# Attention scores for the first batch: four units abreast over six PSUM banks, with masks, maxima and side work put in another order

## The chip, the cores and the metric

The kernel runs on one core of a Trainium2 chip. The metric is the device time of one execution in microseconds (us). Three runs of the kernel before gave 480.39, 482.08 and 484.3 us, with a median of 482.08 us.

## The reference, cut to what matters

The program is one transformer block over 4 batches of 512 tokens of width 256: a modulated layer norm, causal attention with 16 heads of width 16, a gated residual, a second modulated layer norm, and a mixture of 8 experts (one per token) with a shared expert beside them. The change touches the attention of the first batch alone, and what is prepared for the second while it runs:

```python
h = _layernorm(x) * (1 + ca) + sa
qkv = jnp.einsum('bsh,oh->bso', h, Wqkv) + bqkv
scores = jnp.einsum('bhqd,bhkd->bhqk', q, k) * scale      # 16 heads, 512 x 512, causal
scores = jnp.where(causal, -jnp.inf, scores)
attn = jax.nn.softmax(scores, axis=-1)                    # needs each row's maximum
out = jnp.einsum('bhqk,bhkd->bhqd', attn, v)
```

The modulation vectors `sa, ca, ga, sb, cb, gb` are rows of `silu(c) @ wmod`.

## The kernel before, in words

**Two passes over the scores.** The kernel first computes the scores with queries on partitions, only to take each row's maximum (DVE, line 1097). The negated maxima are then written into two spare rows of the stacked queries `qs`, so that a second product, with keys on partitions (`scores_t`, line 1573, matmul at 1592), gives scores minus maximum at once, and ACT takes the exponential (line 872). A *unit* is one PSUM bank of first-pass scores: a query tile t of 128 rows (with 128(t+1) keys), a head i of its group, and m heads in one bank. A group of four heads has 11 units, a batch 4 groups, so 44 units. The first pass runs `LAG` = 33 units ahead of the second.

**The order is written out.** Each engine walks the same loop, `for b in range(-1, B)` and in it `n` from 0 to 43. Stage b = -1 is the head: there the first 33 units of batch 0 are computed by `scores_apart` (line 1517) and nothing of the second pass. Beside them each engine does side work at the steps that the table `HEAD` (line 99) gives, in the order of its own loop. `v` is a projection of V, `turn` the transposes of the next batch's normalised rows, `qk` its four projections of Q and K (units 0 to 3, line 1499), `max` the transpose of the maxima (line 1569) and their negation on DVE (line 1101). `SPLITS` (line 91) says at which step ACT and DVE split a piece of the expert weights into a high and a low half.

**Unstacked products.** For batch 0 the stacked operands arrive late, so `scores_apart` multiplies the four 32-row parts of `qk0` by `qz`, the queries masked to even or odd heads. A mask matmul (L1536, 128x128, all 128 rows) opens each tile and three products of 32 rows (L1541) follow; two units are worked alternately, on different 32-row groups of the array. Units rotate over four banks (`s_bank`, line 275); before a bank is used again, PE waits until DVE has taken the maximum of the unit that was in it (`s_mx`, function `before`, line 279). `query_parity` (line 1257) makes `qz` on DVE, eight instructions (L1261).

**What is precomputed, and where.** PE turns the normalised rows (line 1492). ACT writes them with the modulation as a high half and in f32 (`h_parts`, line 838, L847). POOL subtracts for the low half (`h_low`, line 715, L719). PE projects. ACT writes high half and f32 (`qk_parts`, line 850, L861), and POOL again subtracts (`qk_low`, line 721, L726). `project_qk` waits for both halves of h. PE takes bank M1 for side work in order, each job waiting for the release of the last (`take_bank`, line 1486). POOL works strictly in order too. At steps 30 and 36 of the head it makes the gate rows out of the modulation (`modulation_rows`, line 695, called at line 773), ahead of the side jobs of the same step:

```python
if b < 0 and n in (30, 36):
    modulation_rows(n == 36)
for job, c, k in side_jobs(b, n):      # "turn" -> h_low, "qk" -> qk_low
```

**The SP queue** issues its DMAs in one order, each waiting in front of all behind it. For this stretch the order is:

```python
qk_out(1, 0)          # waits for the high, then the low halves of qk(1,0) and qk(1,1): 6 DMAs
maxima_out(0, 0); maxima(0, 0)
stacks(1, 0)          # waits for qk_out(1, 0) to land: 4 DMAs
qk_out(1, 1); stacks(1, 1)
for k in range(2): halves_out(k); stage_load(k + 3)
```

The first three `stage_load` come ahead of it, and the first of them waits for `s_mp`, since the expert weights overwrite the modulation weights. On ACT, `split_high(2)` (line 911) stands at step 4 of stage b = 0; it waits for the landing of `halves_out(0)` (line 542), which frees its buffer.

Of the kernel before, what the change touches and what calls it, by code (L numbers as in the profile page):

```python
# [20 lines left out]
P = 128  # L21
# [44 lines left out]

def key_units():

    return [(0, i, 1) for i in range(4)] + [(1, i, 1) for i in range(4)] + [(2, 0, 2), (2, 2, 2), (3, 0, 4)]
# [21 lines left out]
SPLITS = {-1: {24: 0, 36: 1},  # L91
# [22 lines left out]
def build(nc, x, wqkvT, bqkv, bqkc, woutT, bout, rwT, gup, down, sgw, suw, sdw, cT, wmod, out):  # L114
    ctx = ExitStack()
    with ctx:
# [158 lines left out]
        def s_bank(N):  # L275

            return [S0, S1, T2, OTb][N % 4] if N < LAG else [T2, S0, S1][N % 3]

        def before(N):

            return max((n + 1 for n in range(max(N - 4, 0), N) if s_bank(n) is s_bank(N)), default=0)
# [40 lines left out]
        s_qz = sem("s_qz")  # L322
        s_tile = sem("s_tile")
# [82 lines left out]
        QU, KU = query_units(), key_units()  # L406
# [57 lines left out]
        def _(sp):  # L464
# [173 lines left out]
        def _(po):  # L638
# [127 lines left out]
            h_low(0, 1)  # L766
            for u in range(4):
# [58 lines left out]
        def _(ac):  # L826
# [118 lines left out]
            def modulation_rows():  # L945
                ac.wait_ge(s_mp, 1)
                ac.wait_ge(s_wl, 1)
                for c, bk in enumerate((T0, T1)):
                    a.activation(mraw[:, 512 * c:512 * (c + 1)], bk[0:B, :], ACT.Copy).then_inc(s_mr, 1)

            for b in range(-1, B):
                for n in range(BU):
# [3 lines left out]
                    if b < 0 and n == 15:  # L956
                        modulation_rows()
# [68 lines left out]
        def _(ve):  # L1026
# [61 lines left out]
            def maxima(N):  # L1088

                b, gr = N // BU, N % BU // UNITS  # L1090
                t, i, m = QU[N % UNITS]
# [165 lines left out]
            def query_parity(f, c):  # L1257

                ve.wait_ge(*((s_ql, 2 * f + 1) if c else (s_qh, 2 * f + 1)))
                for par in range(2):  # L1260
                    v.tensor_scalar(qz[:, c, f, par], qk0[:, c, f], pick[:, par:par + 1], None,  # L1261
                                    ALU.mult).then_inc(s_qz, 1)
# [12 lines left out]
            for c in range(2):  # L1275
                query_parity(1, c)
            for b in range(-1, B):
                for n in range(BU):
# [5 lines left out]
                    if b < 0 and n == 14:  # L1284
                        v.memset(ks[1].rearrange("p h n -> p (h n)").bitcast(F32), ONES).then_inc(s_zero, 1)
                    if b < 0 and n == 22:
# [169 lines left out]
        def _(pe):  # L1456
# [18 lines left out]
            def modulation_rows(c):  # L1475
                pe.wait_ge(s_wmr, 16)
                pe.wait_ge(s_q32, 4)
                for k in range(KC):
                    i = t_.matmul([T0, T1][c][0:B, :], cs[:, 1, k], wm[:, k, 512 * (c + 1):512 * (c + 2)],
                                  start=(k == 0), stop=(k == KC - 1))  # L1480
                if c == 1:
                    i.then_inc(s_mp, 1)
# [34 lines left out]
            def scores_apart(pair):  # L1517

                gr = pair[0] // UNITS
                par, f = gr % 2, gr // 2  # L1520
                t, _, m = QU[pair[0] % UNITS]
                w = P * (t + 1)
                if pair[0] == 0:
                    pe.wait_ge(s_const, 2)
                    pe.wait_ge(s_col, 1)
                if pair[0] % (2 * UNITS) == 0:
                    pe.wait_ge(s_qz, 4 * f + 4)
                    pe.wait_ge(s_ql, 2 * f + 2)
                if max(before(N) for N in pair):
                    pe.wait_ge(s_mx, max(before(N) for N in pair))  # L1530
                for i in range(m):
                    c = slice(w * i, w * (i + 1))
                    if i:
                        pe.wait_ge(s_tile, n_tile[0])
                    for N in pair:
                        t_.matmul(s_bank(N)[:, w * (i + 1) - P:w * (i + 1)], identb[:, :], maskb[:, :],  # L1536
                                  start=(i == 0), stop=False, skip_group_check=True)
                    for p, (cq, ck) in enumerate(((0, 0), (0, 1), (1, 0))):
                        for N in pair:
                            j = 32 * (QU[N % UNITS][1] + i)  # L1540
                            q = t_.matmul(s_bank(N)[:, c], qz[j:j + 32, cq, f, par, P * t:w],  # L1541
                                          qk0[j:j + 32, 2 + ck, f, 0:w], start=False,
                                          stop=(p == 2 and i == m - 1), skip_group_check=True)
                            if p == 2 and i == m - 1:
                                q.then_inc(s_s1, 1)
                    if i < m - 1:
# [26 lines left out]
            def scores_t(N):  # L1573
# [7 lines left out]
                if N == 0:  # L1581
                    pe.wait_ge(s_mr, 2)
# [13 lines left out]
            def values(G, j):  # L1596
# [4 lines left out]
                if j == 0:  # L1601
                    pe.wait_ge(*((s_ote, G) if G else (s_mx, LAG)))
# [102 lines left out]
            for b in range(-1, B):  # L1705
                for n in range(BU):
# [189 lines left out]
```

## Time and profile before

| what | value |
|---|---|
| median of three runs | 482.08 us |
| the profiled execution | 481.26 us |
| its span | 479.5 us |
| PE busy | 414.1 us (86%) |
| DVE busy | 317.1 us (66%) |
| ACT busy | 226.7 us (47%) |
| POOL busy | 210.3 us (44%) |

The span runs from the first to the last instruction of the core; the profiled execution took 1.76 us more than it. Busy time is the union of an engine's instructions. The chain that ended last gives 55% of the span to PE, 17% to DVE, 7% to POOL, 6% to ACT, 5% to DMA and 2% to the SP queue.

### The profile page before, as it was taken

Reading aid. Unit: us, or ns where it says so; the run is one execution under the profiler, and the core shown is the slowest. Engines: PE = TensorE matmul, PEld = TensorE weight load, DVE = VectorE, ACT = ScalarE, POOL = GpSimd, SP = SyncE. Lnnn points to the kernel's source line nnn. Section 1 sums busy time; section 2 is a strip of 40 time slices with the busy share of each in tenths; the row PEclk is TensorE's granted clock in tenths of the full one; section 3 lists DMA queues with packets and bytes.
Section 4 is the critical chain, followed back from the end, with each engine's and each line's share of the span. In section 5 each row is a group of like instructions: output and inputs, shape, how many; then the busy total and the mean of one; then the engine's idle time right before and its main releaser. Section 6 shows DMA issues by size and latency. Waiting matters only on the chain.

```text
span 479.5 us, 8593 instructions
## 1 busy us (share of the span) xinstructions
PE 414.1 (86%) x3009; PEld 230.8 (48%) x3009; DVE 317.1 (66%) x639; ACT 226.7 (47%) x403; POOL 210.3 (44%) x251
## 2 busy tenths in 40 slices
PE   4699983989987888997898969999998999999991
PEld 4234332334544344553443426557655666666661
DVE  3796582966797986899986873497954434444441
ACT  2522441687767575665776554526232332323220
POOL 2491670375232782437541582310240464555332
PEclk9988877799999999998999988999999999999997
DMA  7557358755586665855143101598251344434210
GB/s 245 183 144 199 108 119 243 261 187 170 133 259 232 212 187 136 204 173 176 39 139 125 47 0 45 181 387 310 85 179 45 65 72 91 72 80 73 41 21 0
DMA packets 45921, 67.97 MB, mean 142 GB/s; under 512 B 5364, under 2 KB 33652, under 8 KB 45880
## 3 DMA queue, kind: packets, MB, share of 16 engines
q1 hardware_dynamic: 40200, 58.76, 39.7%
q0 software_dynamic: 5152, 8.14, 8.6%
q8 instruction: 26, 0.43, 0.4%
q10 hardware_dynamic: 528, 0.52, 0.3%
q14 instruction: 15, 0.12, 0.1%
HBM read 43.14 MB, written 25.18 MB: 142 GB/s over the span
## 4 chain that ended last, share of the span: by engine, by line
PE 55%; DVE 17%; POOL 7%; issue 6%; ACT 6%; DMA 5%; SPq 2%; ACTq 0%; DVEq 0%; POOLq 0%
PE bank L1463 35%; PE bank L1608 4%; DVE mx L1097 4%; PE bank L1592 3%; PE bank L1829 2%; DVE rowg L1198 2%; PE bank L1563 2%; PE bank L1541 2%; POOL W L745 2%; ACT W L847 2%; DMA w_d<-rowg 2%; DMA mod_d<-h2T 1%; POOL rowg L753 1%; POOL rowg L752 1%; DMA qk_d<-W 1%
## 5 line engine op out<-in xcount | busy, mean ns | idle before, releaser
L872 ACT ACTIVATE W<-bank 128x512 f32<-128x512 f32 (+1 forms) x176 | 94.8, 563 | 64.4 <-PE bank L1592 62.9
L1097 DVE TENSOR_REDUCE mx<-bank 128x1 f32<-128x384 f32 (+3 forms) x176 | 105.7, 633 | 19.1 <-PE bank L1565 11.3
L1463 PE MATMUL bank<-W 128*128 128x256 f16 (+2 forms) x756 | 107.9, 295 | 8.2 <-POOL W L719 3.6
L1463 PEld LDWEIGHTS bank<-W 128*128 128x128 f16 x756 | 73.6, 100 | 43.5 <-issue 15.2
L745 POOL TENSOR_SCALAR_AFFINE_SELECT W<-W 128x512 f32<-128x512 f32 x64 | 46.0, 721 | 82.3 <-ACT W L872 82.2
L1592 PE MATMUL bank<-W 128*128 128x512 f16 (+3 forms) x256 | 65.1, 312 | 11.5 <-ACT W L872 9.8
L1463 PE MATMUL bank<-W,h2T 128*128 x276 | 67.2, 380 | 1.8 <-DVE W L1213 1.0
L815 POOL DMA_INDIRECT out<-h2T,sidx x23 | 36.3, 1578 | 64.0 <-DVE h2T L1433 63.7
L1563 PE MATMUL bank<-W 126*128 126x128 f16 (+3 forms) x208 | 54.7, 314 | 6.5 <-DVE mx L1097 6.5
L1608 PE MATMUL bank<-W 128*32 128x128 f32 (+3 forms) x512 | 49.1, 457 | 9.1 <-POOL W L745 8.9
L1592 PEld LDWEIGHTS bank<-W 128*128 128x128 f16 x256 | 22.1, 100 | 48.2 <-ACT W L872 24.5
L1463 PE MATMUL bank<-h2T,W 128*128 128x512 f16 x192 | 43.1, 379 | 0.6 <-DVE W L1213 0.6
L1426 DVE TENSOR_TENSOR W<-bank,W 128x512 f16<-128x512 f32 x23 | 15.9, 692 | 37.4 <-ACT W L1010 37.4
L1010 ACT ACTIVATE W<-bank 128x512 f16<-128x512 f32 x23 | 13.7, 597 | 55.1 <-PE bank L1829 55.1
L1463 PEld LDWEIGHTS bank<-W,h2T 128*128 128x128 f16 x276 | 26.4, 97 | 27.2 <-issue 6.3
L1198 DVE SCALAR_TENSOR_TENSOR rowg<-stage,rowg 128x1024 f16<-128x1024 f32 x18 | 24.7, 1374 | 20.4 <-ACT rowg L922 20.4
L801 POOL DMA_INDIRECT rowg<-h_d,gidx x23 | 23.6, 1027 | 31.4 <-DVE gidx L1376 24.7
L1565 PE MATMUL bank<-maskb,identb 128*128 128x128 bf16 (+2 forms) x143 | 36.2, 253 | 0.0
L861 ACT ACTIVATE W<-bank,bqk 128x512 f16<-128x512 f32 (+1 forms) x32 | 20.2, 685 | 21.3 <-PE bank L1463 21.2
L1463 PEld LDWEIGHTS bank<-h2T,W 128*128 128x128 f16 x192 | 18.4, 98 | 21.9 <-DVE W L1213 1.0
L1563 PEld LDWEIGHTS bank<-W 126*128 126x128 f16 x208 | 19.5, 100 | 18.3 <-DVE mx L1097 11.7
L726 POOL TENSOR_TENSOR W<-W 128x512 f16<-128x512 f32 x16 | 19.7, 1233 | 16.1 <-ACT W L861 15.9
(171 smaller groups left out, 561.4 us busy)
## 6 DMA issues: line engine op xcount, KB each, us to landing
w_d<-rowg SPq DMA_DIRECT2D x18, 512.0 KB, 3.5
W<-w_d SPq DMA_DIRECT2D x18, 512.0 KB, 7.9
stage<-in_gup SPq DMA_DIRECT2D x16, 512.0 KB
qk_d<-W SPq DMA_DIRECT2D x48, 128.0 KB
W<-qk_d SPq DMA_DIRECT2D x32, 192.0 KB, 4.2
stage<-in_down SPq DMA_DIRECT2D x8, 512.0 KB
x_sb<-in_x SPq DMA_DIRECT2D x4, 512.0 KB, 9.0
h_d<-gbb SPq DMA_DIRECT2D x4, 512.0 KB, 5.0
```

What stands on the lines that cost most here:

```text
L745: g.affine_select(out=d, in_=d, compare_op=ALU.is_ge, fill=0.0, base=0, pattern=[[0, 4], [1, P]], channel_multiplier=-1).then_inc(s_msk, 1)
L801: g.indirect_dma_start(rowg[:, r % RG, :], None, h2_d, bass.IndirectOffsetOnAxis(ap=gidx[:, r:r + 1].bitcast(U32), axis=0)).then_inc(s_gr[ ...
L815: g.indirect_dma_start(out.rearrange("b s n -> (b s) n"), bass.IndirectOffsetOnAxis(ap=sidx[:, r:r + 1].bitcast(U32), axis=0), ry[r % YR], ...
L861: a.activation(dst, side_bank("qk", b, u)[:, :], ACT.Identity, bias=bqk[:, 2 * isk + u // 2:2 * isk + u // 2 + 1], scale=1.0 / WS if isk e ...
L872: a.activation(PT[j][:, i:i + m, :], t_bank(N)[:, 0:m * w].rearrange("p (i n) -> p i n", i=m), ACT.Exp).then_inc(s_exp, 1)
L1097: v.tensor_reduce(mx_v[:, b % 2, hp0 // 4, par, i:i + m, t], s_bank(N)[:, 0:m * w].rearrange("p (i n) -> p i n", i=m), AX.X, ALU.max).then ...
L1198: v.scalar_tensor_tensor(split_part(k, 1), staged(k), WS, split_part(k, 0), ALU.mult, ALU.subtract).then_inc(s_el, 1)
L1463: i = t_.matmul(outp, l, r, start=(n == 0), stop=(n == len(prods) - 1), **kw)
L1563: t_.matmul(bk[:, w * i:w * (i + 1)], qs[r][0:P - 2, hp, par, P * t:w], ks[r][0:P - 2, hp, 0:w], start=(i == 0), stop=False, skip_group_ch ...
L1565: t_.matmul(bk[:, 0:m * w].rearrange("p (i n) -> p i n", i=m)[:, :, w - P:w], identb[:, :], maskb[:, :].unsqueeze(1).to_broadcast([P, m, P ...
L1592: q = t_.matmul(t_bank(N)[:, w * i:w * (i + 1)], ks[r][:, hp, P * j:P * (j + 1)], qs[r][:, hp, par, P * j:S], start=True, stop=True)
L1608: q = t_.matmul(OTb[32 * i:32 * i + 32, P * j:S], v1[b % 2][:, c:c + 32], PT[j][:, i], start=(j == 0), stop=(j == TT - 1), tile_position=( ...
```

## The change

`ROUNDS` lists, for each of three calls per group, which tile of which unit is computed beside which. `first_units` turns the order of the units of the first 33 around. `scores_apart` takes up to four units at once; its banks are six. The four masked queries of the second half go from DVE to ACT. The rows of modulation go into bank M0, in two calls that stand further apart. Normalisation of batch 1 leaves the `HEAD` table and stands ahead of the loop on DVE, with its POOL part ahead of `qk_low`. Three fills on DVE move. Two splits of weights move later. `max` of the first half of batch 0 moves from step 34 to 32 and the projections of batch 1 from steps 26, 28, 31, 33 to 34, 36, 39, 42. SP's order of DMAs and the steps of POOL's `modulation_rows` are not in the diff.

```diff
+def first_units():
+    return [(t, i, 1) for t in (3, 2) for i in range(4)] + [(1, 0, 2), (1, 2, 2), (0, 0, 4)]
+
+ROUNDS = {0: [[(0, 0), (1, 0), (2, 0), (3, 0)]], 4: [[(4, 0), (5, 0), (6, 0), (7, 0)]],
+          8: [[(8, 0), (9, 0), (10, 1)], [(8, 1), (9, 1), (10, 0)], [(10, 2)], [(10, 3)]]}
-SPLITS = {-1: {24: 0, 36: 1},
-          0: {4: 2, 9: 3, 14: 4, 19: 5, 23: 6},
+SPLITS = {-1: {38: 0},
+          0: {1: 1, 4: 2, 9: 3, 14: 4, 19: 5, 23: 6},
-HEAD = [(12, "stats1", 1, 0), (16, "v", 0, 0), (17, "norm1", 1, 0), (18, "v", 0, 1), (20, "turn", 1, 0),
-        (22, "turn", 1, 1), (26, "qk", 1, 0), (28, "qk", 1, 1), (31, "qk", 1, 2), (33, "qk", 1, 3),
-        (34, "max", 0, 0)]
+HEAD = [(19, "v", 0, 0), (25, "v", 0, 1), (28, "turn", 1, 0), (30, "turn", 1, 1), (32, "max", 0, 0),
+        (34, "qk", 1, 0), (36, "qk", 1, 1), (39, "qk", 1, 2), (42, "qk", 1, 3)]
...
-            return [S0, S1, T2, OTb][N % 4] if N < LAG else [T2, S0, S1][N % 3]
+            return [S0, S1, T2, T0, T1, OTb][N % 6] if N < LAG else SB[N % 3]
...
-            head = {"turn": [M1, M0], "qk": [M1, M0, T0, T1]}
+            head = {"turn": [M1, M0], "qk": [M1, M0, T1, OTb]}
...
                 if k == 0:
-                    sp.wait_ge(s_mp, 1)
+                    sp.wait_ge(s_mp, 2)
...
             h_low(0, 0)
             h_low(0, 1)
+            rstd(ve1, mv1, rs1, 1, s_mv, s_rstd)
             for u in range(4):
                 qk_low(0, u)
...
+            query_parity(0)          # on ACT: four activations with a column as scale
+            query_parity(1)
             for b in range(-1, B):
...
-                    if b < 0 and n == 15:
-                        modulation_rows()
+                    if b < 0 and n == 16:
+                        modulation_rows(0)
+                    if b < 0 and n == 22:
+                        modulation_rows(1)
                         other_high()
...
+            v.memset(qs[0].rearrange("p h two n -> p (h two n)").bitcast(F32), 0.0)
             stats1(0)
             parity_columns()
             norm1(0)
+            v.memset(ks[0].rearrange("p h n -> p (h n)").bitcast(F32), ONES).then_inc(s_zero, 1)
             modulation_columns()
             low_qkv()
-
-            v.memset(qs[0].rearrange("p h two n -> p (h two n)").bitcast(F32), 0.0)
+            v.memset(ks[1].rearrange("p h n -> p (h n)").bitcast(F32), ONES).then_inc(s_zero, 1)
+            stats1(1)
+            norm1(1)
             ve.wait_ge(s_pick, 1)
-            query_parity(0, 0)
-            v.memset(ks[0].rearrange("p h n -> p (h n)").bitcast(F32), ONES).then_inc(s_zero, 1)
-            query_parity(0, 1)
-            for c in range(2):
-                query_parity(1, c)
+            query_parity(0)
+            query_parity(1)
...
-                    if b < 0 and n == 22:
+                    if b < 0 and n == 36:
                         low_others()
...
+                rounds = [[(N0 - N0 % UNITS + u, i) for u, i in r] for r in ROUNDS[N0 % UNITS]]
+                units = [N for N, _ in rounds[0]]
...
+                if max(before(N) for N in units):
+                    pe.wait_ge(s_mx, max(before(N) for N in units))
+                left = {N: score_unit(N)[2] for N in units}
+                for k, r in enumerate(rounds):
+                    if k:
                         pe.wait_ge(s_tile, n_tile[0])
+                    for N, i in r:
                         t_.matmul(s_bank(N)[:, w * (i + 1) - P:w * (i + 1)], identb[:, :], maskb[:, :],
...
                     for p, (cq, ck) in enumerate(((0, 0), (0, 1), (1, 0))):
+                        for N, i in r:
...
+                            q = t_.matmul(s_bank(N)[:, w * i:w * (i + 1)], qz[j:j + 32, cq, f, par, P * t:w],
+                                          qk0[j:j + 32, 2 + ck, f, 0:w], start=False, stop=done, skip_group_check=True)
...
                 if N == 0:
-                    pe.wait_ge(s_mr, 2)
+                    pe.wait_ge(s_mx, LAG - 3)
...
                     if 0 <= N < LAG:
-                        if N % UNITS == 0:
-                            scores_apart([N])
-                        elif N % UNITS % 2:
-                            scores_apart([N, N + 1])
+                        if N == 0:
+                            scores_apart(0)
+                        if N % UNITS == 1:
+                            scores_apart(N + 3)
+                        elif N % UNITS == 5:
+                            scores_apart(N + 3)
+                        elif N % UNITS == 9 and N + 2 < LAG:
+                            scores_apart(N + 2)
...
-                    if b < 0 and n in (12, 14):
-                        modulation_rows(n == 14)
+                    if b < 0 and n in (14, 20):
+                        modulation_rows(n == 20)
```

## Rows read from the trace of the kernel before

**Rows 1.** The timeline of PE (start us, us, engine, line, operation), after the head.

```profile
66.50 0.61 PE L1592 MATMUL bank<-W 128*128 128x512 f16 x1
...
83.00 0.50 PE L1592 MATMUL bank<-W 128*128 128x384 f16 x1 [7.62 <-ACT W L872]
```

**Rows 2.** The timeline of ACT, the high half of weight piece 2.

```profile
81.51 1.06 ACT L922 ACTIVATE rowg<-stage 128x1024 f16<-128x1024 f32 x1 [9.72 <-DMA w_d<-rowg]
```

**Rows 3.** The timeline of SP's queue, its DMA issues.

```profile
32.34 3.67 SPq L488 DMA_DIRECT2D qk_d<-W  x6
39.60 1.77 SPq L505 DMA_DIRECT2D W<-qk_d  x4
...
52.66 3.65 SPq L488 DMA_DIRECT2D qk_d<-W  x6
61.12 0.34 SPq L515 DMA_DIRECT2D ng_d<-negm  x1
...
65.08 3.66 SPq L488 DMA_DIRECT2D qk_d<-W  x6
73.71 1.77 SPq L505 DMA_DIRECT2D W<-qk_d  x4
75.53 0.44 SPq L544 DMA_DIRECT2D w_d<-rowg  x1
```

**Rows 4.** The timeline of POOL in the head.

```profile
53.29 1.15 POOL L726 TENSOR_TENSOR W<-W 128x512 f16<-128x512 f32 x1 [2.35 <-ACT W L861]
54.38 0.39 POOL L699 COPY h2T<-h2T 4x256 f32<-4x256 f32 x1
...
60.97 3.34 POOL L726 TENSOR_TENSOR W<-W 128x512 f16<-128x512 f32 x2
...
68.54 0.71 POOL L708 TENSOR_TENSOR h2T<-h2T 4x256 f32<-4x256 f32 x1
```

**Rows 5.** The timeline of PE in the head.

```profile
15.86 7.59 PE L1463 MATMUL bank<-W 128*128 128x512 f16 x24 [3.35 <-POOL W L719]
...
26.68 0.28 PE L1536 MATMUL bank<-maskb,identb 128*128 128x128 bf16 x2
...
27.33 3.54 PE L1479 MATMUL bank<-stage,cs 128*4 128x512 f32 x4
...
31.61 1.88 PE L1479 MATMUL bank<-stage,cs 128*4 128x512 f32 x4
...
35.55 0.28 PE L1536 MATMUL bank<-maskb,identb 128*128 128x128 bf16 x2
...
36.56 1.48 PE L1463 MATMUL bank<-W 128*128 128x256 f16 x12
...
39.58 0.66 PE L1496 MATMUL bank<-ident,W 128*128 128x128 f32 x4 [0.67 <-DVE W L1064]
...
45.68 2.72 PE L1463 MATMUL bank<-W 128*128 128x512 f16 x6 [0.25 <-POOL W L719]
```

**Rows 6.** Busy time by window: stretch, length, engines (instructions), granted clock, DMA share, GB/s.

```profile
28.00:30.00 2.00, 2.00 (x4) 0.26 (x2) 2.00 (x6) 0.00 (x0) 1.94 (x2) 0.50 0.11 24
```

**Rows 7.** The timeline of DVE in the head.

```profile
4.37 1.41 DVE L1039 BATCH_NORM_STATS2 st<-x_sb 128x6 f32<-128x256 f32 x4 [4.37 <-DMA x_sb<-in_x]
...
14.02 3.47 DVE L1270 MEMSET W<- 128x4096 f32 x1 [0.80 <-issue]
...
35.75 0.76 DVE L1064 SCALAR_TENSOR_TENSOR W<-bank,W 128x256 f32<-128x256 f32 x2 [0.47 <-PE bank L1463]
...
39.44 1.88 DVE L1097 TENSOR_REDUCE mx<-bank 128x1 f32<-128x512 f32 x3
...
49.57 1.95 DVE L1097 TENSOR_REDUCE mx<-bank 128x1 f32<-128x384 f32 x4
```

**Rows 8.** The timeline of ACT in the head.

```profile
40.27 1.45 ACT L847 ACTIVATE W<-bank,sac,cac 128x512 f16<-128x512 f32 x2 [5.06 <-PE bank L1496]
...
51.94 1.26 ACT L861 ACTIVATE W<-bank,bqk 128x512 f16<-128x512 f32 x2 [2.24 <-PE bank L1463]
```

More of the change, by code:

```diff
@@ L275, in s_bank @@
         def s_bank(N):
-            return [S0, S1, T2, OTb][N % 4] if N < LAG else [T2, S0, S1][N % 3]
+            return [S0, S1, T2, T0, T1, OTb][N % 6] if N < LAG else SB[N % 3]
         def before(N):
-            return max((n + 1 for n in range(max(N - 4, 0), N) if s_bank(n) is s_bank(N)), default=0)
+            return max((n + 1 for n in range(max(N - 6, 0), N) if s_bank(n) is s_bank(N)), default=0)
         def qk_halves(b):
@@ L322, in build @@
         s_qz = sem("s_qz")
+        s_qz1 = sem("s_qz1")
         s_tile = sem("s_tile")
@@ L943, in _, with modulation_rows, query_parity @@
                 qk_parts(0, u)
[L945 to L949, printed above, removed]
+            def modulation_rows(c):
+                ac.wait_ge(s_mp, c + 1)
+                if c == 0:
+                    ac.wait_ge(s_wl, 1)
+                a.activation(mraw[:, 512 * c:512 * (c + 1)], M0[0:B, :], ACT.Copy).then_inc(s_mr, 1)
+            def query_parity(c):
+                ac.wait_ge(s_pick, 1)
+                ac.wait_ge(*((s_ql, 3) if c else (s_qh, 3)))
+                for par in range(2):
+                    a.activation(qz[:, c, 1, par], qk0[:, c, 1], ACT.Copy, scale=pick[:, par:par + 1]).then_inc(s_qz1, 1)
+            query_parity(0)
+            query_parity(1)
             for b in range(-1, B):
@@ L1475, in modulation_rows @@
             def modulation_rows(c):
-                pe.wait_ge(s_wmr, 16)
-                pe.wait_ge(s_q32, 4)
+                if c == 0:
+                    pe.wait_ge(s_wmr, 16)
+                    pe.wait_ge(s_q32, 2)
+                else:
+                    pe.wait_ge(s_mr, 1)
                 for k in range(KC):
-                    i = t_.matmul([T0, T1][c][0:B, :], cs[:, 1, k], wm[:, k, 512 * (c + 1):512 * (c + 2)],
+                    i = t_.matmul(M0[0:B, :], cs[:, 1, k], wm[:, k, 512 * (c + 1):512 * (c + 2)],
                                   start=(k == 0), stop=(k == KC - 1))
-                if c == 1:
-                    i.then_inc(s_mp, 1)
+                i.then_inc(s_mp, 1)
             last_job = []
@@ L1524, in scores_apart @@
                     pe.wait_ge(s_const, 2)
                     pe.wait_ge(s_col, 1)
[L1526 to L1533, printed above, removed]
+                    pe.wait_ge(s_qz, 3)
@@ new lines, in scores_apart @@
+                    pe.wait_ge(s_ql, 2)
+                elif N0 == 4:
+                    pe.wait_ge(s_q32, 4)
+                elif N0 == UNITS:
+                    pe.wait_ge(s_qz, 4)
+                elif N0 == 2 * UNITS:
+                    pe.wait_ge(s_qz1, 4)
+                    pe.wait_ge(s_ql, 4)
+                if max(before(N) for N in units):
[3 more added lines that the diff above has]
+                    if k:
@@ L1534, in scores_apart @@
                         pe.wait_ge(s_tile, n_tile[0])
-                    for N in pair:
+                    for N, i in r:
+                        t, _, m = score_unit(N)
+                        w = P * (t + 1)
                         t_.matmul(s_bank(N)[:, w * (i + 1) - P:w * (i + 1)], identb[:, :], maskb[:, :],
-                                  start=(i == 0), stop=False, skip_group_check=True)
+                                  start=(left[N] == m), stop=False, skip_group_check=True)
@@ L1538, in scores_apart @@
                     for p, (cq, ck) in enumerate(((0, 0), (0, 1), (1, 0))):
[L1539 to L1544, printed above, removed]
+                        for N, i in r:
+                            t, i0, m = score_unit(N)
+                            w, j = P * (t + 1), 32 * (i0 + i)
+                            done = p == 2 and left[N] == 1
+                            q = t_.matmul(s_bank(N)[:, w * i:w * (i + 1)], qz[j:j + 32, cq, f, par, P * t:w],
+                                          qk0[j:j + 32, 2 + ck, f, 0:w], start=False, stop=done, skip_group_check=True)
+                            if p == 2:
+                                left[N] -= 1
+                            if done:
@@ L1545, in scores_apart @@
                                 q.then_inc(s_s1, 1)
-                    if i < m - 1:
+                    if k + 1 < len(rounds):
                         n_tile[0] += 1
@@ L1601, in values @@
                 if j == 0:
-                    pe.wait_ge(*((s_ote, G) if G else (s_mx, LAG)))
+                    pe.wait_ge(*((s_ote, G) if G else (s_mx, LAG - 3)))
                 pe.wait_ge(s_msk, 4 * G + j + 1)
```

22 lines of the change are left out of this document (10 added, 12 removed).

## The prediction, made before the changed kernel ran

> **What bounds the kernel now.** The whole change lies in the first 70 us, so the question is not how busy an engine is over the span but what the work after the head waits for. I read PE's timeline first. PE starts the second pass of scores at 66.50 and then stops for 7.62 us, until 83.00, for an exponential of ACT [rows 1]. ACT's timeline shows why: at step 4 of stage b = 0 it stands in front of `split_high(2)` for 9.72 us, and the releaser is a DMA, the landing of `halves_out(0)` [rows 2]. So I followed SP's queue backwards [rows 3]. `halves_out(0)` is issued at 75.53, right behind `stacks(1,1)`, which waited for `qk_out(1,1)` to land (68.74 to 73.71, 4.97 us). That one was issued from 65.08, behind `stacks(1,0)` and the maxima. Ahead of all that stands a slack: the six issues of `qk_out(1,0)` ended at 56.31, and the queue then sat until 61.12 for the negated maxima. **The head therefore pays only through the time at which `halves_out(0)` is issued.** If PE finishes the head sooner and that issue does not move, its stop of 7.6 us only grows.
>
> **The tail of the chain.** The diff leaves SP's order alone, but turns what waits around: maxima are made ahead of the projections of batch 1, and SP still wants `qk_out(1,0)` first. Call L the time at which POOL ends `qk_low(1,1)`. In the kernel before, L = 53.29 + 1.15 = 54.44 [rows 4]. Behind L come, from the rows of SP [rows 3]: the two low issues of `qk_out(1,0)`, 2 x 3.65/6 = 1.2; the wait for its landing ahead of `stacks(1,0)`, taken as 39.60 - 36.01 = 3.6; its four issues 1.8; `qk_out(1,1)` 3.66; its landing 4.97; the four issues of `stacks(1,1)` 1.8. Together 17.0. The maxima go out meanwhile. So L + 17.0 is the issue of `halves_out(0)`, and the break-even is L = 75.53 - 17.0 = 58.5. The 4.8 us of slack are spent first; each microsecond beyond is lost at the end, since ACT, PE and the next DMAs resume from that landing.
>
> **PE up to the turn of batch 1.** PE ends the first projections at 15.86 + 7.59 = 23.45 [rows 5] and the scores begin there. The prices: a pair of 512 wide units takes 36.56 - 35.55 = 1.01, of which the two masks are 0.22 by the next line's start. Four abreast cost two more masks, 1.23 in all, if the four 32-row groups truly run together; if only two do, 2.0. The trace shows pairs alone, so both ends stay in the range; I take 1.23, since in a pair two products take the time of one (six of 512 in about 0.75). Four 384 wide units: 1.23 less three steps of 0.05, 1.07. The call at unit 8 has two rounds of three tiles and two of one; a round of two tiles is 27.33 - 26.68 = 0.65, so 2 x 0.76 + 2 x 0.65 = 2.8. A group's PE work is 5.1.
>
> DVE pays for a group 7 x 0.63 + 4 x 0.49 = 6.4 [rows 7], more than PE. Walked in order, with six banks: units 0 to 3 end at 24.8; units 6 and 7 want two maxima, so the second call runs 26.2 to 27.3. The first modulation rows took 3.54, the second 1.88, the same four instructions [rows 5]; the granted clock was 0.50 under the first, the 1.2 GHz level, after a stretch of 32-row products [rows 6]. The new order has the same kind of work ahead of it: I take 3.5 and keep 1.9 for the low end. To 30.8; unit 8's call to 33.65; V (1.48) to 35.1. DVE does V's eviction at step 19, between maxima 8 and 9, so it had stood since 32.9; with it 35.8 (0.76 for two [rows 7]), and maximum 12 ends at 38.25. PE has meanwhile done the call at unit 11 (to 36.35) and the second rows (38.2), and goes on to 39.4, V to 40.85. DVE evicts to 41.55, maximum 15 is at 42.05, and unit 19's call runs 42.2 to 45.05. **turn(1,0) starts at 45.05; it was 39.58 [rows 5].**
>
> This is where a rule of the Trainium skill can be weighed. "TensorEngine Tiling (Array Packing)", section "PSUM Bottleneck", says that tiling speeds TensorE up and not the emptying of PSUM, which may become the bound. The 6.4 against 5.1 of the rows agree. With PE's work alone (18.6 up to here) the turn would come at 42.15 and not at 45.05, 2.9 us less in every number below.
>
> **From the turn to L.** turn 0.65, ACT 1.45 [rows 8], `h_low(1,0)` 1.15: 48.3. Now POOL meets step 30, where `modulation_rows(0)` stands ahead of `h_low(1,1)` of the same step. It takes 60.97 - 54.38 = 6.6 [rows 4]; before, it stood behind both turns and both projections that SP wants. To 54.9; `h_low(1,1)` to 56.05. PE has by then turned, done the calls at 22 and 26 and the transpose of the maxima, and waits from 52.45 on. qk(1,0) starts at 56.2; it takes 1.45 at full clock and 2.72 at half [rows 5], I take the middle, 58.3. ACT 1.26 [rows 8] to 59.55, `qk_low(1,0)` to 60.7. At step 36 the same again: `modulation_rows(1)` ahead of `qk_low(1,1)`, from 64.3 (two low halves behind 60.97) to 69.25, 4.95 [rows 4]. To 65.65; **L = 66.8**. qk(1,1) itself is done long before.
>
> **The sum.** L is 8.3 past the break-even of 58.5, `halves_out(0)` goes at 83.8 and not at 75.53, PE resumes near 91.3. On the profiled execution's 481.26 us that is 489.6; against the median of 482.08 (0.8 higher) 490.4. I say 490.0, +1.7%.
>
> **What I cost at nothing.** The four ACT copies of `qz` have no row; the nearest are 0.63 each [rows 8], 2.5 from 24.8 on, and their reader, unit 22, comes at 47.8; without that cover they would cost 2.5. The fill of 3.47 in front of `stats1(0)` fits into the 4.37 that DVE waits for x [rows 7]; its start isn't shown, and up to 0.5 could leak into everything (0 to 0.5, 0 taken). The fill of `ks[1]` and the norm of batch 1 lie under PE's projections until 23.45; if x of batch 1 came late, `qk_low(0,0)` on POOL would wait behind its `rstd` (0 to 1). `stage_load(0)` now waits for both modulation rows, at 38.2, and SP passed `stacks(0,1)` at 41.4: nothing. `scores_t(0)` wants maxima 30: nothing, as the negated maxima leave SP only near 68 and PE starts the second pass near 74 to 76, still ahead of ACT's stop. Split 1 moves to stage b = 0, step 1: 1.06 of ACT inside that stop. A gain from any of these is excluded, as none of them stands on the chain.
>
> **Rivals.**
> - **POOL's rows are not in the way**, the rest as above, because they are out of the path by some overlap I miss. Then turn(1,1) at 47.15, `h_low(1,1)` 50.4, qk(1,0) after unit 26 at 52.45, L = 59.1: +0.6, 482.7 us. For it: ACT and PE have the inputs by then. Against: POOL works in order, and rows 4 show `qk_low` standing behind the same arithmetic at 60.97. With DVE's waits smaller and full clock too, but POOL in the way, L = 61.5: +3.0, 484.5; that too is under 1%.
> - **The other side: the faster head reaches SP.** If neither DVE's maxima nor POOL's arithmetic hold it, PE's work alone gives turn(1,0) at 42.15, `h_low(1,1)` at 47.5, qk(1,1) to 51.8 and L = 54.3: -4.2, 477.9 us. It decides from L under 58.5. For it: PE's own work in the head falls by some 2.4 us a group. Against: both holds are in the order of the code.
> - **Worse than forecast.** Four abreast run as two pairs (0.8 and 0.6 a group), PE's waits of 3.7 us bring the half clock for both projections, and the first landing takes 5.0 and not 3.6: +11 to +14, 493 to 496.
>
> **How the numbers follow.** Forecast 0.62; worse 0.12; one of the two middling outcomes 0.20; faster 0.06. About 1% (4.8 us) is what a measurement of this kernel can tell from no change. Forecast and worse are slower by over 1%, with 0.02 of them short of it: 0.72. Faster by over 1% is a part of the last: 0.04. The rest is within 1%: 0.24. The range starts at the middling outcome with POOL in the way, 484.5, and reaches to 495.
>
> **What would show it.** In the trace after: POOL's gate rows (L704 to L708 of before) directly between the two `h_low` of batch 1, and again between its first two `qk_low`; PE idle ahead of qk(1,0), released by POOL's `h_low`; SP without its wait for the negated maxima, but waiting for ACT and POOL ahead of `qk_out(1,0)`; `halves_out(0)` near 84 and PE's second stop ending near 91. `halves_out(0)` at 77 or earlier makes the prediction wrong; so does a stop of PE that ends where it did although L is late, which would mean that ACT waits for something else.

## The result, and the profile after

The changed kernel took 490.5 us (median of four runs, 488.87 to 494.06) against 483.19 us of the kernel before beside it (also four, 480.39 to 484.37), a ratio of 1.017 with a 95% interval of 1.0095 to 1.0245. Five more rounds on another chip, on which both kernels were slower, gave 496.97 against 487.92, ratio 1.018 (1.0134 to 1.0225). The change makes the kernel 1.8% slower. The profiled execution took 489.97 us, its span is 488.2 us. In all ratios, here and below, runs over 1.5% above the fastest of their kernel are left out, and in the medians they are not.

The timeline of POOL after, in the head, answers to [rows 4]:

```profile
45.94 1.16 POOL L732 TENSOR_TENSOR W<-W 128x512 f16<-128x512 f32 x1 [10.76 <-ACT W L861]
47.04 0.39 POOL L712 COPY h2T<-h2T 4x256 f32<-4x256 f32 x1
...
52.76 0.71 POOL L721 TENSOR_TENSOR h2T<-h2T 4x256 f32<-4x256 f32 x1
53.55 1.15 POOL L732 TENSOR_TENSOR W<-W 128x512 f16<-128x512 f32 x1
58.95 1.15 POOL L739 TENSOR_TENSOR W<-W 128x512 f16<-128x512 f32 x1 [4.25 <-ACT W L875]
60.07 1.08 POOL L717 TENSOR_SCALAR h2T<-h2T 4x256 f32<-4x256 f32 x1
...
64.32 1.43 POOL L721 TENSOR_TENSOR h2T<-h2T 4x256 f32<-4x256 f32 x1
65.83 1.15 POOL L739 TENSOR_TENSOR W<-W 128x512 f16<-128x512 f32 x1
```

L732 is `h_low`, L739 `qk_low`, and the lines between (L712 to L721) are the gate rows. They lie between the two `h_low` of batch 1, 47.04 to 53.47, and again between its first two `qk_low`. Before the first they find POOL idle for 10.76 us. L, the end of `qk_low(1,1)`, is 65.83 + 1.15 = 66.98.

The timeline of PE after answers to [rows 5] and [rows 1]:

```profile
24.47 0.38 PE L1569 MATMUL bank<-maskb,identb 128*128 128x128 bf16 x4
24.78 0.83 PE L1576 MATMUL bank<-W 32*128 32x512 f16 x12
27.07 0.38 PE L1569 MATMUL bank<-maskb,identb 128*128 128x128 bf16 x4 [1.46 <-DVE mx L1122]
...
27.98 1.88 PE L1505 MATMUL bank<-stage,cs 128*4 128x512 f32 x4
...
43.71 0.66 PE L1521 MATMUL bank<-ident,W 128*128 128x128 f32 x4
...
51.05 0.40 PE L1569 MATMUL bank<-maskb,identb 128*128 128x128 bf16 x4 [1.88 <-DVE mx L1122]
...
54.85 2.72 PE L1486 MATMUL bank<-W 128*128 128x512 f16 x6 [2.81 <-POOL W L732]
58.93 2.74 PE L1486 MATMUL bank<-W 128*128 128x512 f16 x6 [1.36 <-ACT W L875]
...
67.53 1.47 PE L1486 MATMUL bank<-W 128*128 128x512 f16 x6 [1.36 <-ACT W L875]
72.70 0.44 PE L1628 MATMUL bank<-W 128*128 128x512 f16 x1 [3.71 <-DMA W<-ng_d]
...
91.52 0.50 PE L1628 MATMUL bank<-W 128*128 128x384 f16 x1 [10.53 <-ACT W L886]
```

Twelve products on four row groups take 0.83. In the kernel before, six on two row groups took 0.82, so the scores do run four abreast. PE nevertheless starts the first projection of batch 1 at 54.85 and not at 45.68, released by POOL's `h_low`. It waits for the negated maxima at 72.70, and its stop for ACT, 7.62 before, is 10.53.

The timeline of SP's queue after answers to [rows 3], and that of ACT to [rows 2]:

```profile
62.42 5.78 SPq L501 DMA_DIRECT2D qk_d<-W  x6
68.24 0.47 SPq L528 DMA_DIRECT2D ng_d<-negm  x1
70.56 0.56 SPq L535 DMA_DIRECT2D W<-ng_d  x2
71.24 1.76 SPq L518 DMA_DIRECT2D W<-qk_d  x4
73.04 3.66 SPq L501 DMA_DIRECT2D qk_d<-W  x6
82.36 1.77 SPq L518 DMA_DIRECT2D W<-qk_d  x4
84.17 0.44 SPq L557 DMA_DIRECT2D w_d<-rowg  x1
```

```profile
90.03 1.06 ACT L936 ACTIVATE rowg<-stage 128x1024 f16<-128x1024 f32 x1 [12.51 <-DMA w_d<-rowg]
```

From `qk_out(1,0)` on there is no slack left; it spreads over 5.78 since its last two issues wait for L. `halves_out(0)` goes at 84.17 instead of 75.53, 8.64 later, and PE resumes 8.52 later (91.52 against 83.00). Behind that point nothing changed: from the end of PE's stop to the end of the span it is 396.7 us after and 396.5 before. PE's busy time fell from 414.1 to 406.9 us, and the kernel is slower.

### The profile page after: what moved, and what is told of

It is laid out like the page before. It is cut to its first block, busy times and chain, and to the rows that moved or that the text cites. A ratio compares the mean times of both kernels' runs of the same rounds, so it can differ in the third digit from the quotient of the medians.

```text
span 488.2 us, 8596 instructions
## 1 busy us (share of the span) xinstructions
PE 406.9 (83%) x3009; PEld 229.5 (47%) x3009; DVE 312.1 (64%) x635; ACT 229.1 (47%) x407; POOL 210.3 (43%) x251
## 4 chain that ended last, share of the span: by engine, by line
PE 52%; DVE 18%; POOL 11%; issue 6%; ACT 5%; DMA 5%; SPq 2%; ACTq 0%; DVEq 0%; POOLq 0%
PE bank L1486 35%; DVE mx L1122 4%; PE bank L1644 4%; PE bank L1628 3%; PE bank L1869 2%; POOL W L758 2%; DVE rowg L1223 2%; PE bank L1599 2%; ACT W L861 2%; DMA w_d<-rowg 1%; DMA mod_d<-h2T 1%; DMA qk_d<-W 1%; POOL rowg L765 1%; POOL W L739 1%; POOL rowg L766 1%
## 5 line engine op out<-in xcount | busy, mean ns | idle before, releaser
L886 ACT ACTIVATE W<-bank 128x512 f32<-128x512 f32 (+1 forms) x176 | 94.6, 563 | 59.1 <-PE bank L1628 57.5
L758 POOL TENSOR_SCALAR_AFFINE_SELECT W<-W 128x512 f32<-128x512 f32 x64 | 47.1, 738 | 85.1 <-ACT W L886 85.0
L936 ACT ACTIVATE rowg<-stage 128x1024 f16<-128x1024 f32 x18 | 19.0, 1055 | 12.8 <-DMA w_d<-rowg 12.8
```

Source lines behind the costliest of these rows:

```text
L758: g.affine_select(out=d, in_=d, compare_op=ALU.is_ge, fill=0.0, base=0, pattern=[[0, 4], [1, P]], channel_multiplier=-1).then_inc(s_msk, 1)
L886: a.activation(PT[j][:, i:i + m, :], t_bank(N)[:, 0:m * w].rearrange("p (i n) -> p i n", i=m), ACT.Exp).then_inc(s_exp, 1)
```

## The experiments

Ratios are to the kernel before in the same call. It took 482.46 us beside the kernels with gate rows between, gate rows last, maxima first and splits late, and 482.15 us beside the four that follow them in the table. L, the issue of `halves_out(0)` and the end of PE's stop come from each run's own profiled execution.

| kernel | us | ratio (95%) | L | halves_out(0) | stop ends | span less that |
|---|---|---|---|---|---|---|
| before | | 1 | 54.4 | 75.53 | 83.00 | 396.5 |
| after | 490.5 | 1.017 (1.0095 to 1.0245) | 67.0 | 84.17 | 91.52 | 396.7 |
| before, gate rows between | 488.52 | 1.011 (1.0081 to 1.014) | 63.7 | 82.21 | 89.69 | 396.5 |
| after, gate rows last | 486.22 | 1.0059 (1.0028 to 1.009) | 62.7 | 81.39 | 88.75 | 398.6 |
| after, maxima first | 489.21 | 1.0114 (1.006 to 1.0169) | 66.9 | 83.31 | 90.77 | 396.5 |
| after, splits late | 489.38 | 1.013 (1.0077 to 1.0183) | 66.4 | 83.89 | two stops | |
| before, halves first | 483.87 | 1.0025 (0.9999 to 1.005) | 56.3 | 67.12 | 97.94 | 386.0 |
| before, chain open | 475.03 | 0.9839 (0.9797 to 0.9882) | 55.7 | 66.35 | none | |
| after, three edits | 488.17 | 1.012 (1.0067 to 1.0172) | 62.9 | 80.39 | 87.97 | 396.8 |
| after, three edits, chain open | 484.84 | 1.0019 (0.9985 to 1.0052) | 65.5 | 72.52 | none by ACT | |
| after, gate rows early | 491.77 | 1.0088 (1.0056 to 1.012) | 61.1 | 79.66 | 87.21 | 401.9 |
| the same, chain open | 481.46 | 0.9877 (0.9856 to 0.9898) | 60.7 | 67.41 | none | |
| after, again | 496.97 | 1.018 (1.0134 to 1.0225) | 68.7 | 86.10 | 93.53 | 403.1 |

The last three ran where the kernel before took 487.8 to 487.9.

### Before, gate rows between: the suspected cost alone

```diff
-                    if b < 0 and n in (30, 36):
-                        modulation_rows(n == 36)
+                    if b < 0 and n in (22, 28):
+                        modulation_rows(n == 28)
```

> The kernel before with one line changed: POOL makes the gate rows at steps 22 and 28 instead of 30 and 36, so that they stand ahead of h_low(1,1) and ahead of qk_low(1,1), where they stand in the changed kernel. Theory (POOL's order sets L, the end of qk_low(1,1), and 58.5 is the break-even): h_low(1,1) ends 6.5 later, qk(1,0) starts near 51 instead of 45.7, L comes near 64 to 65 instead of 54.4, halves_out(0) at 81 to 82 instead of 75.5, and the time is 5 to 7 us above before, about 488. Rival 1 (the new order of scores, banks and projections is what costs, POOL's rows are covered): no more than 1 us above before, 482 to 483. Rival 2 (all of L's delay is paid, there is no slack in SP's queue): +10.

Measured 488.52, ratio 1.011. Rival 1 is refuted: with not one instruction of the scores changed, POOL's order costs 5 to 6 us. POOL's timeline in this run:

```profile
41.95 1.15 POOL L719 TENSOR_TENSOR W<-W 128x512 f16<-128x512 f32 x1 [6.08 <-ACT W L847]
43.05 0.92 POOL L699 COPY h2T<-h2T 4x256 f32<-4x256 f32 x1
...
51.02 1.15 POOL L719 TENSOR_TENSOR W<-W 128x512 f16<-128x512 f32 x1
...
62.58 2.26 POOL L726 TENSOR_TENSOR W<-W 128x512 f16<-128x512 f32 x2
```

`h_low(1,1)` ends at 52.2 instead of 45.5, and L is the first of the two at 62.58, so 63.7, 9.3 later than before. `halves_out(0)` moved by 6.7 only, which refutes rival 2 as well. SP's timeline shows that the cost does not pass through L here:

```profile
59.43 5.51 SPq L488 DMA_DIRECT2D qk_d<-W  x6
67.89 0.34 SPq L515 DMA_DIRECT2D ng_d<-negm  x1
```

The six issues end at 64.94, and the queue still stands 2.95 for the negated maxima (4.8 before). From the issue of the maxima to `halves_out(0)` it is 14.3 here and 14.4 before. POOL's rows reach the queue through PE: it waits for `h_low(1,1)`, does the scores behind qk(1,0) later, and transposes the maxima at 66.67 instead of 59.90, 6.8 later.

### After, gate rows last: the suspected cost taken away

```diff
-                    if b < 0 and n in (30, 36):
-                        modulation_rows(n == 36)
...
+                    if b < 0 and n == 43:
+                        modulation_rows(0)
+                        modulation_rows(1)
```

> The changed kernel with POOL's two pieces of gate rows moved behind all low halves of batch 1 (step 43 of the head). Theory: h_low(1,1) ends near 50, qk(1,0) starts near 52 behind unit 26's call instead of 54.85, L is 59 to 61 instead of 67.0, halves_out(0) at 76 to 78.5 instead of 84.2, time 6 to 8 us below the changed kernel, about 483, level with before. Rival 1 (order of scores and projections costs by itself): no more than 2 us gained, 488 or more. Rival 2 (the faster head pays once POOL is out of the way): under 479.

Measured 486.22, ratio 1.0059 against 1.017 and 1.018: some 5 to 6 us came back, less than the 6 to 8 expected. That is more than rival 1 allows and far from rival 2. The expected "level with before" was missed: the interval lies above 1. POOL's and PE's timelines say where part of the rest is:

```profile
61.55 1.16 POOL L739 TENSOR_TENSOR W<-W 128x512 f16<-128x512 f32 x1 [2.95 <-ACT W L876]
```

```profile
27.81 3.27 PE L1506 MATMUL bank<-stage,cs 128*4 128x512 f32 x4
...
53.91 2.16 PE L1487 MATMUL bank<-W 128*128 128x512 f16 x6
57.43 2.74 PE L1487 MATMUL bank<-W 128*128 128x512 f16 x6 [1.36 <-ACT W L876]
```

L is 62.7 and not 59 to 61. The first modulation rows took 3.27 here (1.88 in the changed kernel's profile), and the second turn stood 1.92 later. The first two projections took 2.16 and 2.74, where they take 1.47 at the full clock. L is also no longer what SP waits for: its six issues run without a break from 60.92, released by ACT's high halves. What else the order of scores and projections costs is not taken apart.

### After, maxima first: what the title promises

```diff
-            qk_out(1, 0)
             maxima_out(0, 0)
             maxima(0, 0)
+            qk_out(1, 0)
             stacks(1, 0)
```

> The changed kernel with SP's two maxima DMAs of the first half ahead of qk_out(1,0), as the title of the change has it. Theory (only the issue of halves_out(0) counts): the second pass of scores starts near 69 instead of 72.7, as PE has its maxima when the projections end; halves_out(0) moves by 0 to 0.7 earlier, since the landing of qk_out(1,0) is waited for anyway; PE's stop for ACT grows by about 3; the time falls by 0 to 1 us, 489.5 to 490.5. Rival (the late maxima are what costs): the 3.7 us of PE's wait for them come back, about 487.

Measured 489.21, ratio 1.0114, whose interval overlaps that of the changed kernel. PE's timeline:

```profile
68.73 0.38 PE L1628 MATMUL bank<-W 128*128 128x512 f16 x1
...
72.16 0.39 PE L1628 MATMUL bank<-W 128*128 128x512 f16 x1 [2.06 <-ACT W L886]
...
90.77 0.50 PE L1628 MATMUL bank<-W 128*128 128x384 f16 x1 [11.51 <-ACT W L886]
```

The wait for the maxima is gone and the second pass starts at 68.73, as expected (69). But its third product waits for ACT until 72.16: ACT's work on the last projection and its table load for the exponential (1.28, to 71.5) stand there, which I had not priced. `halves_out(0)` is 0.86 earlier, PE's stop 0.98 longer, and it ends 0.75 earlier (90.77 against 91.52) with the same 396.5 behind it. The times alone can't tell the two apart, since the rival's 487 (ratio 1.009) lies in the interval too. In the profile the 3.7 us of the wait did not come back; the stop took them.

### After, splits late: where ACT meets the chain

```diff
-          0: {1: 1, 4: 2, 9: 3, 14: 4, 19: 5, 23: 6},
+          0: {1: 1, 10: 2, 13: 3, 16: 4, 19: 5, 23: 6},
```

> The changed kernel with weight pieces 2, 3 and 4 split at steps 10, 13 and 16 of stage b = 0 instead of 4, 9 and 14, so that ACT meets the wait for halves_out(0) six steps later. Theory (that wait is the only thing through which the head is paid): PE works on through steps 4 to 9, its stop of 10.5 us shrinks to about 4, the time falls by 5 to 7 us to about 484.5. Rival (the DMA chain itself is the bound, the next stop takes over, as later pieces, maxima or stacks come just as late): under 2 us gained.

Measured 489.38, ratio 1.013; I expected 484.5, and the rival (under 2 us gained) is the nearer one: against 1.017 the ratio gives 1.9 us, within the intervals. ACT's timeline:

```profile
90.11 1.06 ACT L936 ACTIVATE rowg<-stage 128x1024 f16<-128x1024 f32 x1 [5.89 <-DMA w_d<-rowg]
...
101.87 1.06 ACT L936 ACTIVATE rowg<-stage 128x1024 f16<-128x1024 f32 x1 [3.99 <-DMA w_d<-rowg]
```

The stop was cut in two, and the second piece stands for piece 4, which waits for `halves_out(2)`. The two waits together are 9.9, 2.6 less than the one wait of 12.5. So the landing of `halves_out(0)` is not the only gate.

### Before, halves first, and before, chain open: which gate carries the end

```diff
             stacks(1, 0)
+            for k in range(2):
+                halves_out(k)
+                stage_load(k + 3)
             qk_out(1, 1)
             stacks(1, 1)
-            for k in range(2):
-                halves_out(k)
-                stage_load(k + 3)
```

> The kernel before with SP's halves_out(0), stage_load(3), halves_out(1), stage_load(4) moved ahead of qk_out(1,1). It asks what PE's stop for ACT is worth by itself. Theory A (the prediction's, that the issue of halves_out(0) alone carries the end): halves_out(0) goes near 65, it lands before ACT's step 4, the stop of 7.6 is gone and the time falls by 6 to 8 us, to about 475. Theory B (the whole chain of SP carries it: the landing of the modulation rows in front of halves_out(2), and piece 4 behind that): the first stop is gone, but mod_d goes at 78 as before, halves_out(2) at 85 to 86 as before, ACT meets its wait at step 14 instead, and the gain is 0 to 1.5 us.

Measured 483.87, ratio 1.0025. `halves_out(0)` went 8.4 earlier and nothing was gained: Theory A, the one my prediction stood on, falls as a statement about that DMA alone, and the gain is within what Theory B allows. SP's and ACT's timelines:

```profile
83.34 0.34 SPq L573 DMA_DIRECT2D mod_d<-h2T  x1
88.38 0.34 SPq L511 DMA_DIRECT2D W<-mod_d  x1
...
89.23 0.50 SPq L544 DMA_DIRECT2D w_d<-rowg  x1
```

```profile
80.00 1.05 ACT L922 ACTIVATE rowg<-stage 128x1024 f16<-128x1024 f32 x1
96.45 1.06 ACT L922 ACTIVATE rowg<-stage 128x1024 f16<-128x1024 f32 x1 [10.97 <-DMA w_d<-rowg]
```

SP waits for the modulation rows to land (83.34 to 88.38) with `halves_out(2)` behind it, and ACT stops for piece 4 instead of piece 2. The edit was not free, which I had not expected: `qk_out(1,1)`, now behind the halves, took 7.2 to land (4.97 before), `mod_d` went 5.1 later than before and `halves_out(2)` 3.3 later. That a second gate carries the end is therefore shown only by the second kernel, which opens it too. (`FIRST` gives the pieces that are sent later; it starts at 4, as 2 and 3 now go here.) The edit against the kernel with halves first:

```diff
             qk_out(1, 1)
+            sp.wait_ge(s_m4, 1)
+            sp.dma_start(mod_d[:, :], m4[:, :]).then_inc(s_md, 16)
+            halves_out(2)
+            stage_load(5)
             stacks(1, 1)
-            sp.wait_ge(s_m4, 1)
-            sp.dma_start(mod_d[:, :], m4[:, :]).then_inc(s_md, 16)
+            halves_out(3)
+            stage_load(6)
             sp.wait_ge(s_md, 16)
...
-FIRST = [(2, 4, 7), (7, 10, 13), (13, 15, 18)]
+FIRST = [(4, 4, 7), (7, 10, 13), (13, 15, 18)]
```

> The same, and the modulation rows sent before halves_out(2), with their landing waited for only behind halves_out(2), stacks(1,1) and halves_out(3). Theory B: now neither landing stands in front of a piece that ACT waits for; halves_out(2) near 75, no stop over 3 us at steps 4 or 14, 4 to 7 us below before, about 476 to 478. Theory A: the same as with halves_out(0) and (1) moved alone. Rival C (DMA bandwidth or PE itself takes over): under 2 us below before.

Measured 475.03, ratio 0.9839: **7 us faster than the kernel before**, a little under the expected 476 to 478 and the best of all kernels here. The changed kernel's median, in another call, was 490.5, some 15 us more. SP's and PE's timelines:

```profile
66.35 0.44 SPq L544 DMA_DIRECT2D w_d<-rowg  x1
...
73.33 0.50 SPq L572 DMA_DIRECT2D mod_d<-h2T  x1
76.17 0.34 SPq L544 DMA_DIRECT2D w_d<-rowg  x1
```

```profile
94.86 0.39 PE L1596 MATMUL bank<-W 128*128 128x512 f16 x1 [0.87 <-DMA W<-ng_d]
```

Two landings were taken out from in front of DMAs that ACT depends on; no wait of PE over 1.2 us is left between 66 and 110. Rival C (something else takes over at once) is refuted.

### After, with the edits together

The gate rows last and the maxima first are the edits of above; the third moves DVE's fills. First the three together:

```diff
+            maxima_out(0, 0)
+            maxima(0, 0)
             qk_out(1, 0)
...
-            v.memset(qs[0].rearrange("p h two n -> p (h two n)").bitcast(F32), 0.0)
             stats1(0)
...
             low_qkv()
-            v.memset(ks[1].rearrange("p h n -> p (h n)").bitcast(F32), ONES).then_inc(s_zero, 1)
+            v.memset(qs[0].rearrange("p h two n -> p (h two n)").bitcast(F32), 0.0).then_inc(s_zero, 1)
...
             query_parity(1)
+            v.memset(ks[1].rearrange("p h n -> p (h n)").bitcast(F32), ONES).then_inc(s_zero, 1)
```

> The changed kernel with three edits: POOL's gate rows behind the low halves of batch 1 (as tried alone), SP's first maxima ahead of qk_out(1,0) (as tried alone), and DVE's long fill behind low_qkv instead of ahead of the first statistics. Theory (each acts on the same chain and they add): 4.3 of the first, about 1 of the second, 0.7 of the third, so 6 below the changed kernel, 484.5, still 2 above before, since the projections of batch 1 stand behind 8 more units of scores than before. Rival (all loss was in these three): level with before or under it, 482 or less.

Measured 488.17, ratio 1.012, a miss by 3.7. The ratio can't be told from that with the gate rows last alone (1.0028 to 1.009). PE's timeline shows the third edit backfire:

```profile
28.85 0.38 PE L1570 MATMUL bank<-maskb,identb 128*128 128x128 bf16 x4 [2.28 <-DVE mx L1123]
```

The second call of scores starts at 28.85 and not 27.07: the fills now stand in front of the first maxima. The second turn stands at 50.01, 2.2 later than with the gate rows last alone (47.83). The first two projections ran at the full clock here (1.47 each), so L came out alike, 62.9. That the fills ate the other gains is likely, and no run shows it alone.

The second kernel adds the opened chain of SP. It is near that of above, not the same: only `halves_out(0)` goes ahead of `qk_out(1,1)`, and `halves_out(1)` behind it.

> The three edits on the changed kernel and the opened SP chain together (halves_out(0) ahead of qk_out(1,1), the modulation rows sent early and waited for late). Theory: once the SP chain is not the bound, the change's shorter scores (5.1 instead of 7.5 us of PE a group) can count, though DVE's 6.4 a group takes most of it and the projections are later; 476 to 480, within 2 us of the same opening on the kernel before. Rival (the head's order still costs): 482 or more.

Measured 484.84, ratio 1.0019, above the 476 to 480 expected; the rival's 482 or more came out. With the gate rows last on POOL, `mod_d` could only go at 85.55, where SP had waited 6.9 for it, and it held `halves_out(2)` behind it; the mask of the probabilities, also on POOL, held PE:

```profile
86.39 1.93 PE L1650 MATMUL bank<-W 128*32 128x512 f32 x8 [4.72 <-POOL W L763]
```

So I tried the changed kernel with POOL's rows in idle stretches, without the moved fills:

```diff
-                    if b < 0 and n in (30, 36):
-                        modulation_rows(n == 36)
+                    if b < 0 and n in (27, 33):
+                        modulation_rows(n == 33)
```

> The changed kernel with one line of POOL changed: the gate rows stand at steps 27 and 33 of the head, ahead of h_low(1,0) and ahead of qk_low(1,0), into two stretches in which POOL sat idle in the changed kernel (35.2 to 45.9, and from 50 on). Theory (POOL's order is what the change lost by): L comes 5 to 6 earlier than 67.0, near 61 to 62, limited by PE's wait for DVE's maxima and the half clock, halves_out(0) near 79; 485 to 486, that is 4 to 5 under the changed kernel and 3 above before. Rival (a placement that is wholly hidden is worth more than one at the end, as nothing of it is left in front of the masks): 483 or less.

On this chip the kernel before took 487.77, so only the ratio can be read: 1.0088 against 1.018 for the changed kernel on an equally slow chip. The one line gives back half of the loss, about 4.5 us, as expected (4 to 5), and L is 61.1. SP's six issues again run without a break, from 59.32, released by ACT. This kernel with the chain opened in the same way as the last:

> The same, with SP's maxima first, halves_out(0) ahead of qk_out(1,1), the modulation rows sent early and waited for late. No fill is moved and the gate rows are ready near 55, the two things that held back the kernel with three edits and the opened chain. Theory: with SP's chain open the second pass starts near 69 to 71, 2.5 to 4 later than in the kernel before (66.5) and runs on; 477 to 480, which is 2 to 5 above the opened chain on the kernel before (475.0). Rival (once the chain is open, the shorter scores pay): 475 or less.

Ratio 0.9877, against 0.9839 for the opened chain on the kernel before: the intervals (0.9856 to 0.9898, 0.9797 to 0.9882) overlap, and the difference of 0.0038 is 1.8 us, on the side expected but not shown. PE's timeline:

```profile
64.86 0.38 PE L1633 MATMUL bank<-W 128*128 128x512 f16 x1
...
68.30 0.39 PE L1633 MATMUL bank<-W 128*128 128x512 f16 x1 [2.07 <-ACT W L891]
```

The second pass starts at 64.86, earlier than the 69 to 71 expected and 3.1 earlier than in the opened chain on the kernel before (67.95). The lead is gone 20 us later: PE transposes the next maxima at 83.92 against 83.70. In between its third product waits 2.07 for ACT, and ACT stands 2.19 and 1.86 for the landings of weight halves, waits that the kernel before with its chain opened does not have. So the new order did bring the second pass forward here, and the time does not show it; that these waits took the lead back is likely, and no run takes them away.

### The changed kernel again

> The changed kernel itself, unedited, in five more rounds beside the kernel before, to narrow the interval of 1.0095 to 1.0245 that four runs gave: 1.013 to 1.020 if the first ratio stands. The profile shows how far L, the issue of halves_out(0) and the end of PE's stop vary from run to run: within 2 us of 67.0, 84.2 and 91.5, with the granted clock under the modulation rows as the likeliest cause of a difference.

Ratio 1.018, within what was expected. L was 68.7, `halves_out(0)` came at 86.10 and the stop ended at 93.53, 1.7 to 2.0 past the first profile. The first modulation rows took 3.06 here and 1.88 there, and turn(1,0) starts at 44.97.

## Why the prediction was right, step by step

**The time**: 490.0 forecast, 490.5 measured, the cause as forecast. POOL's gate rows between the low halves are shown from both sides: put into the old order they cost 1.1%, moved within the new one they give back 0.9 to 1.2%. That is about 5 of the 8 us lost. The sum put nearly all of the loss on them: without them it had L = 59.1 and +0.6. Measured with them out of the way, L is 62.7 or 61.1 and the ratio 1.006 to 1.009.

**L and what hangs on it**: L = 66.8 forecast, 66.98 measured; `halves_out(0)` 83.8 and 84.17; PE resumes at 91.3 and 91.52. Part of this is luck, since errors inside cancelled:
- turn(1,0): 45.05 forecast, 43.71 measured, although the scores began at 24.47 and not 23.45. The half clock that I took for the first modulation rows was not there: 1.88 and not 3.5. It came later. The profile's windows of the changed kernel:

```profile
28.00:30.00 2.00, 2.00 (x11) 0.42 (x7) 2.00 (x5) 0.24 (x2) 1.94 (x2) 1.00 0.24 81
...
54.00:56.00 2.00, 1.15 (x3) 0.43 (x4) 0.00 (x0) 0.00 (x0) 0.70 (x1) 0.50 0.00 0
```

  The granted clock was 1.00 (2.4 GHz) where it had been 0.50 [rows 6], and 0.50 (1.2 GHz) under the first projections of batch 1, after PE had stood idle for 2.81: 2.72 and not the 2.1 taken. In the second profile of the same kernel the first modulation rows did take 3.06, and L was 68.7.
- The fill ahead of the statistics: costed at nothing, with up to 0.5 to leak. DVE's timeline shows 0.7:

```profile
1.72 3.47 DVE L1289 MEMSET W<- 128x4096 f32 x1 [1.72 <-PEq L1926]
5.10 1.34 DVE L1064 BATCH_NORM_STATS2 st<-x_sb 128x6 f32<-128x256 f32 x4
```

  DVE starts at 1.72, which the trace of before did not show, and the statistics begin at 5.10 and not 4.37 [rows 7].
- The second gate rows took 5.7 (60.07 to 65.75) and not 4.95.
- Behind L it was 17.2 and not 17.0. The 3.6 for the landing of `qk_out(1,0)` were 3.0, and SP stood for the landing of the maxima in them; the landing of `qk_out(1,1)` took 5.66 and not 4.97.
- The middling rival's 484.5 does not follow from its +3.0: on the median of 482.08 that is 485.1.

**DVE against PE**: four abreast made a call 1.14, I had 1.23. PE's waits for DVE's maxima over 0.4 are 1.46, 0.45, 1.31 and 1.88, together 5.1. The rule that emptying PSUM may become the bound once TensorE is tiled (the Trainium skill, "TensorEngine Tiling (Array Packing)", section "PSUM Bottleneck") agrees with these rows.

**Costed at nothing, and nothing**: ACT's copies, `stage_load(0)`, split 1. The later maxima cost 0.75 at PE's stop by the profile with maxima first; its time alone does not settle it.

**What failed**: "the head pays only through the time at which `halves_out(0)` is issued". It gave the right number since the change shifts everything on SP alike: `halves_out(0)` by 8.64, `mod_d` (78.23 to 86.88) and `halves_out(2)` (85.98 to 94.63) by 8.65. Moving the first alone gained nothing; taking `mod_d`'s landing out from in front of `halves_out(2)` as well gained 7 us. L as the one time that sets that issue holds for the changed kernel: L rose 12.5 and `halves_out(0)` 8.6, a slack of 3.9, and the sum had used 4.1 (58.5 - 54.4). It does not hold for three others: with the gate rows between in the old order the maxima set it, and with them last or early ACT's high halves start the six issues, so from L to `halves_out(0)` it is 18.7 and 18.6 instead of 17.2.

**Left open**: how the remaining cost of the new order (ratio about 1.006 to 1.009 with the gate rows out of the way) divides between the projections standing behind eight more units, the fill on DVE and the half clock. No run took one of these alone.

## What to carry to other kernels

Where a queue holds its DMAs in order, find which landing the next busy engine needs and walk back from there; a stage that gets faster pays only if that issue moves. Moving steps on one engine moves them against what another engine does at the same step: the steps of POOL's gate rows, which the diff did not touch, cost about 5 us here, and 7 us less work of PE did not reach the end. When a wait is taken away and nothing is gained, look for the next landing in the same queue: taking out both gave 1.6%. Look, too, at what released the first of a queue's issues: it need not be the input that you had in mind.

## What the runs showed of the hardware

- Four row groups of 32 work in parallel: twelve products of 512 columns in 0.83 us, six on two row groups in 0.82. The masks, on all rows, add about 0.1 each (the products start 0.31 behind four, 0.21 behind two).
- Between the end of six `qk_d` writes and the read that needs them, SP stood 2.2 us (maxima first) to 5.9 (gate rows last), and 7.2 where weight halves and loads had been issued in between (halves first).
- The 16 KB of maxima landed 1.4 to 1.7 us after their issue with nothing sent just ahead, 2.3 to 3.1 right behind the six writes, 2.3 to 2.4 at 49.7 us, where the DMA engines were still busy, and 5.9 at 86.9 us in the kernel before with its chain opened.
- The level of TensorE's clock under the same instructions differed from run to run: the first modulation rows of the changed kernel took 1.88 us in one profile and 3.06 in another of the same kernel, with a granted clock of 1.00 and of 0.50 from 28 to 30 us.
